# Membrane recursion of a spiking delta-rule layer: from one pass behind the front into the delta loop

## The reference, cut to what matters

```python
def step(carry, ins):
    s, mem = carry
    qt, kt, vt, dt, at, bt = ins
    mem = DECAY * mem + dt                      # DECAY 0.9
    sg = jax.nn.sigmoid(SBETA * (mem - THR))
    hard = (mem > THR).astype(mem.dtype)        # THR 0.5
    spike = sg + jax.lax.stop_gradient(hard - sg)
    mem = mem - spike * THR
    alpha = jax.nn.sigmoid(at + asp * spike)
    beta = jax.nn.sigmoid(bt[..., None] + jnp.sum(spike * bsp, -1, keepdims=True))
    active = (jnp.sum(jnp.abs(spike), -1, keepdims=True) > 0).astype(qt.dtype)
    ...
```

## Time and profile before

| | us |
|---|---|
| median of three runs | 3083.59 |
| the profiled run's own time | 3076.32 |
| its span, first to last instruction | 3074.5 |
| PE busy in the span | 2411.1 (78%) |
| DVE busy | 1566.4 (51%) |
| ACT busy | 994.6 (32%) |
| POOL (GpSimd) busy | 675.6 (22%) |

### The profile page before, as it was taken

How to read it: one execution, slowest core, us unless ns; L and a number is a source line. 1 busy time by engine, 2 the same in 40 slices (tenths; PEclk the granted TensorE clock), 3 DMA queues, 4 the chain that set the end, 5 groups by cost and what they waited for, 6 DMA issues and landing times. The chain is left out here.

```text
span 3074.5 us, 73508 instructions
## 1 busy us (share of the span) xinstructions
PE 2411.1 (78%) x31207; PEld 1690.7 (55%) x31207; DVE 1566.4 (51%) x3747; ACT 994.6 (32%) x1934; POOL 675.6 (22%) x816
## 2 busy tenths in 40 slices
PE   7999889997676530888989898988888868856665
PEld 4666666666655210255656565655566747555553
DVE  4555555554622567364555464636363722584333
ACT  3343443433122530324343434343434332301111
POOL 1000101000044400141313140404040300204553
PEclk9898998987599765789999999999999985556555
DMA  3000000000111102000000000000000011000113
GB/s 142 8 8 1 8 8 5 1 1 1 66 34 34 61 21 120 31 3 19 6 19 6 19 6 19 6 19 6 16 6 2 7 41 46 2 28 29 37 36 104
DMA packets 43654, 79.45 MB, mean 26 GB/s; under 512 B 6116, under 2 KB 27372, under 8 KB 40516
## 3 DMA queue, kind: packets, MB, share of 16 engines
q1 hardware_dynamic: 36292, 60.30, 5.6%
q0 software_dynamic: 7040, 14.43, 1.7%
HBM read 48.56 MB, written 26.15 MB: 24 GB/s over the span
## 5 line engine op out<-in xcount | busy, mean ns | idle before, releaser
L2582 POOL TENSOR_TENSOR delta_scaled_beta_k<-delta_scaled_beta_k,delta_decays 128x256 f32<-128x256 f32 x160 | 124.2, 776 | 537.0 <-DVE weights_sb L2683 363.5
L2661 DVE COPY_PREDICATED delta_neg_a_and_p_t<-delta_level_int,bank 128x256 f32<-128x256 uint8 x384 | 179.6, 538 | 88.5 <-PE bank L2204 87.3
L2228 PEld LDWEIGHTS bank<-delta_inverse,delta_neg_a_and_p_t 64*64 64x64 f32 x5120 | 186.7, 152 | 45.7 <-issue 45.2
L2228 PE MATMUL bank<-delta_inverse,delta_neg_a_and_p_t 64*64 64x64 f32 x5120 | 210.0, 240 | 0.0
L2432 ACT ACTIVATE delta_two_less_ax<-bank 128x512 f32<-128x512 f32 x160 | 94.8, 597 | 248.8 <-PE bank L2228 248.7
L303 PE MATMUL bank<-attn_z_self_t,weights_sb 128*128 128x256 f32 x512 | 149.3, 442 | 14.9 <-DVE attn_cross_values L741 11.2
L2204 PE MATMUL bank<-weights_sb,delta_scaled_beta_k 64*64 64x64 f32 x6144 | 127.7, 228 | 40.2 <-DVE delta_neg_a_and_p_t L2661 35.5
L2204 PEld LDWEIGHTS bank<-weights_sb,delta_scaled_beta_k 64*64 64x64 f32 x6144 | 110.4, 140 | 76.5 <-DVE delta_neg_a_and_p_t L2661 52.3
L683 POOL TENSOR_TENSOR attn_probs<-attn_probs,attn_row_sum 128x512 f32<-128x512 f32 x64 | 65.4, 1043 | 390.6 <-DVE attn_row_sum L766 390.6
L312 PE MATMUL bank<-attn_w_value_out,attn_z_self_t 128*64 128x512 f32 x512 | 144.8, 692 | 2.1 <-DVE attn_z_value_out L706 1.4
L2250 PE MATMUL bank<-delta_two_less_ax,delta_inverse_t 64*64 64x64 f32 x4096 | 133.4, 218 | 3.4 <-issue 3.2
(11 more groups left out here) (508 smaller groups left out, 5527.3 us busy)
## 6 DMA issues: line engine op xcount, KB each, us to landing
delta_spikes<-front_drive SPq DMA_DIRECT2D x8, 1024.0 KB, 8.7
weights_sb<-delta_spikes SPq DMA_DIRECT2D x8, 1024.0 KB, 5.0
weights_sb<-in_w_moe_dram SPq DMA_DIRECT2D x1, 4352.0 KB, 15.3
z_rows<-moe_z_all SPq DMA_DIRECT2D x16, 256.0 KB, 2.3
weights_sb<-moe_outs SPq DMA_DIRECT2D x8, 512.0 KB, 7.2
weights_sb<-in_w_delta_dram SPq DMA_DIRECT2D x1, 2816.0 KB, 9.9
weights_sb<-in_ctx_tok_dram SPq DMA_DIRECT2D x8, 264.0 KB, 5.6
attn_x_channels<-in_x_dram SPq DMA_DIRECT2D x8, 256.0 KB, 3.0
```

The lines of the kernel that those rows point to most:

```text
L2228: last = pe.matmul(out_[rows(sg), u], AP[rows(sg), hp, eo, b4, 0, :], X[rows(sg), hp, u], start=False, stop=True, skip_group_check=True)
L2582: pool.tensor_tensor(r_[:, :, 0, :], r_[:, :, 0, :], a_[:, :, 1, 0:1].to_broadcast([128, T // (2 * c), c]), ALU.mult)
L2661: last = dve.copy_predicated(second(AP[:, hp, eo, :, :, :].rearrange("p b i n -> p (b i) n"), c), m_, PAIR[hp % 2][eo][:, :].rearrange("p ...
```

## The change

The recursion of groups 0 and 1 stays in the front, cut into pieces of 13 time steps that DVE runs behind the convolutions of groups 3 to 7, on 128 x 64 elements. The spikes of group 0 stay in SBUF, those of group 1 go to DRAM. Of the other six groups the front writes the drive itself to DRAM, while it runs. The delta stage loads it two iterations ahead, and in iteration `it` DVE steps the membrane of group `it + 2`, on 128 x 32 elements, in five pieces: 26, 14, 10, 7 and 7 time steps. GpSimd turns the result to spikes behind its last scale. There are two tiles for spikes in place of one, and `kr` has one buffer in place of two.

```diff
-                mem = sb("membrane", [128, NG * HDP * GB], ctx=ctx)
+                mem = sb("membrane", [128, 2 * HDP * GB], ctx=ctx)
...
+                        if g >= 3:
+                            sp.wait_ge(s["drive"], HDP * g)
+                            sp.dma_start(drive_rows[g - 1, :, :, :], drive_of(g - 1)).then_inc(drive_out[(g - 1) % 2], 16)
+                    sp.wait_ge(s["drive"], HDP * NG)
+                    sp.dma_start(drive_rows[NG - 1, :, :, :], drive_of(NG - 1)).then_inc(drive_out[(NG - 1) % 2], 16)
+                    sp.wait_ge(s["spikes"], 2)
+                    sp.dma_start(drive_rows[1, :, :, :], drive_of(1)).then_inc(s["spikes_out"], 16)
...
                             act.wait_ge(s["drive_ps"], HDP * g + j + 1)
-                            act.activation(drive[:, g, j, :], bank[6 + j % 2][:, :], ACT.Copy, scale=2.0).then_inc(s["drive"], 1)
+                            if g >= 4:
+                                act.wait_ge(drive_out[g % 2], 16 * (g // 2 - 1))
+                            act.activation(drive_of(g)[:, j, :], bank[6 + j % 2][:, :], ACT.Copy, scale=2.0).then_inc(s["drive"], 1)
...
-                    dve.wait_ge(s["drive"], NG * HDP)
-                    dr = drive[:, :, :, :].rearrange("p g j (b t) -> p (g j b) t", t=S)
-                    for t in range(S):
-                        m_ = dr[:, :, t]
-                        if t >= 1:
-                            link(dve.scalar_tensor_tensor(m_, mem[:, :], -0.9, m_, ALU.mult, ALU.add))
-                        if t < S - 1:
-                            link(dve.scalar_tensor_tensor(mem[:, :], m_, 1.0, m_, ALU.is_gt, ALU.subtract))
-                    for g in range(NG):
-                        dve.tensor_scalar(drive[:, g, :, :], drive[:, g, :, :], 1.0, None, ALU.is_gt).then_inc(s["spikes"], 1)
+                        if g >= 3:
+                            dve.wait_ge(s["drive"], 2 * HDP)
+                            for t in range(13 * (g - 3), min(13 * (g - 2), S)):
+                                membrane(t)
+                    dve.tensor_scalar(spk0, drive_of(0), 1.0, None, ALU.is_gt).then_inc(s["spikes"], 1)
+                    dve.tensor_scalar(drive_of(1), drive_of(1), 1.0, None, ALU.is_gt).then_inc(s["spikes"], 1)
...
+                    def load_drive(g):
+                        if g >= 2:
+                            sp.wait_ge(s["bt_ps"], nth_of("bt", g - 2, 3))
+                            sp.wait_ge(s["al_rd"], nth_of("al", g - 2, 3))
+                        sp.dma_start(SPK[g % 2][:, :, :], drive_rows[g, :, :, :]).then_inc(s[f"drive_in{g % 2}"], 16)
...
                         out_ = fill("ct", g, j)
-                        pe.wait_ge(s["spikes_in"], 16 * (g + 1))
-                        pe.matmul(out_[:, :], BLOCKSUM, spk[:, j, :], start=True, stop=True).then_inc(s["ct_ps"], 1)
+                        if g == 1:
+                            pe.wait_ge(s["drive_in1"], 16)
+                        elif g >= 2:
+                            pe.wait_ge(s["spikes"], g - 1)
+                        pe.matmul(out_[:, :], BLOCKSUM, SPK[g % 2][:, j, :], start=True, stop=True).then_inc(s["ct_ps"], 1)
...
+                    def spikes(g):
+                        pool.wait_ge(s["potential"], g - 1)
+                        pool.tensor_scalar(SPK[g % 2][:, :, :], SPK[g % 2][:, :, :], 1.0, None, ALU.is_gt).then_inc(s["spikes"], 1)
...
                             scale(it, 4)
+                            if it + 2 < NG:
+                                spikes(it + 2)
...
+                    def membrane(g, t0, t1):
+                        dve.wait_ge(s[f"drive_in{g % 2}"], 16 * (g // 2 + g % 2))
+                        rows_ = SPK[g % 2].rearrange("p h (b t) -> p (h b) t", t=S)
+                        for t in range(t0, t1):
+                            m_ = rows_[:, :, t]
+                            if t == S - 1:
+                                dve.scalar_tensor_tensor(m_, mem[:, :], -0.9, m_, ALU.mult, ALU.add).then_inc(s["potential"], 1)
+                            elif t >= 1:
+                                link(dve.scalar_tensor_tensor(m_, mem[:, :], -0.9, m_, ALU.mult, ALU.add))
+                            if t < S - 1:
+                                link(dve.scalar_tensor_tensor(mem[:, :], m_, 1.0, m_, ALU.is_gt, ALU.subtract))
...
+                        drive = core and it + 2 < NG
+                        if drive:
+                            membrane(it + 2, 0, 26)
                         if tail:
                             t_hidden(it - 1, 0)
...
                         if front:
                             f_bc("bk", it + 1)
+                        if drive:
+                            membrane(it + 2, 26, 40)
                         if tail:
                             t_hidden(it - 1, 2)
...
                         if front:
                             f_bc("bq", it + 1)
+                        if drive:
+                            membrane(it + 2, 40, 50)
+                        if front:
                             f_ct(it + 1, 0)
+                        if drive:
+                            membrane(it + 2, 50, 57)
                         if tail:
                             t_out(it - 1)
+                        if drive:
+                            membrane(it + 2, 57, S)
```

More of the change, by code:

```diff
@@ L1940, in z_rms, with membrane @@
                         last.then_inc(s["z_rms"], 1)
+                    two = drive[:, 0:2, :, :].rearrange("p g j (b t) -> p (g j b) t", t=S)
+                    def membrane(t):
+                        m_ = two[:, :, t]
+                        if t >= 1:
+                            link(dve.scalar_tensor_tensor(m_, mem[:, :], -0.9, m_, ALU.mult, ALU.add))
+                        if t < S - 1:
+                            link(dve.scalar_tensor_tensor(mem[:, :], m_, 1.0, m_, ALU.is_gt, ALU.subtract))
                     z_rms(0)
@@ L1956, in _ @@
                         last.then_inc(s["conv"], 1)
-                    dve.wait_ge(s["drive"], NG * HDP)
-                    dr = drive[:, :, :, :].rearrange("p g j (b t) -> p (g j b) t", t=S)
-                    for t in range(S):
-                        m_ = dr[:, :, t]
-                        if t >= 1:
-                            link(dve.scalar_tensor_tensor(m_, mem[:, :], -0.9, m_, ALU.mult, ALU.add))
-                        if t < S - 1:
-                            link(dve.scalar_tensor_tensor(mem[:, :], m_, 1.0, m_, ALU.is_gt, ALU.subtract))
-                    for g in range(NG):
-                        dve.tensor_scalar(drive[:, g, :, :], drive[:, g, :, :], 1.0, None, ALU.is_gt).then_inc(s["spikes"], 1)
+                        if g >= 3:
[4 more added lines that the diff above has]
+                    dve.tensor_scalar(drive_of(1), drive_of(1), 1.0, None, ALU.is_gt).then_inc(s["spikes"], 1)
             run_stage("front", "bias_row pads gate_w var log_var guessed rstd z_rms z z_rms_ps z_ps z_rms_t z_t g1_ps gate_hidden g2_ps gate conv h "
-                               "h_out0 h_out1 gate_out0 gate_out1 drive_ps drive spikes spikes_out dve", body)
+                               "h_out0 h_out1 gate_out0 gate_out1 drive_out0 drive_out1 drive_ps drive spikes spikes_out dve", body)
         def delta():
@@ L2009, in body @@
                 spare = region[0][:, 11 * 512:]
-                spk = spare[:, 0:HDP * T].rearrange("p (h t) -> p h t", h=HDP)
+                spk1 = sb("odd_spikes", [128, HDP, T], ctx=ctx)
+                SPK = (spare[:, 0:HDP * T].rearrange("p (h t) -> p h t", h=HDP), spk1)
+                mem = sb("membrane", [128, HDP * GB], ctx=ctx)
                 zt = spare[:, HDP * T:HDP * T + T].rearrange("p (i d) -> p i d", d=128)
                 y2 = spare[:, HDP * T + T:HDP * T + 2 * T].rearrange("p (i d) -> p i d", d=128)
-                kr = sb("scaled_beta_k", [128, 2, HDP, T], ctx=ctx)
+                kr = sb("scaled_beta_k", [128, HDP, T], ctx=ctx)
                 al = sb("decays", [128, 2, HDP, T], ctx=ctx)
@@ L2083, in _ @@
                             load_h(g + 3)
-                        if g + 2 < NG:
-                            load_spikes(g + 2)
+                        if g + 3 < NG:
+                            load_drive(g + 3)
                         load_gate(g + 1)
@@ L2190, in diag @@
                                 t = slice(b * S, b * S + S)
-                                last = pe.matmul(two[eo][rows(sg), b4 * 64:b4 * 64 + 64], kr[r, g % 2, hp, t], kq[r, g % 2, 1, hp, t],
+                                last = pe.matmul(two[eo][rows(sg), b4 * 64:b4 * 64 + 64], kr[r, hp, t], kq[r, g % 2, 1, hp, t],
                                                  start=b < 2, stop=True, skip_group_check=True)
@@ L2203, in products @@
                                 t = slice(b * S, b * S + S)
-                                last = pe.matmul(two[eo][rows(sg), b4 * 64:b4 * 64 + 64], kr[r, g % 2, hp, t],
```

(3 more changed lines are left out.)

38 lines of the change are left out of this document (21 added, 17 removed).

## The result

The changed kernel takes 2987.51 us in the median of four runs (2981.93 to 2989.48), the kernel before 3078.35 us on the same chip; the ratio is 0.970 (95% interval 0.967 to 0.972). Measured twice more, each time against the kernel before on the same chip, the ratio was 0.968 (0.962 to 0.973) and 0.968 (0.964 to 0.971); the three pairs of medians lie 91, 103 and 99 us apart. The forecast was 2980 us, range 2960 to 3015. The profiled run took 2981.93 us; its forecast was 2979.

The account below looks back on a forecast made before the run. It took the recursion to stand alone on the path and the delta stage to be PE's, with DVE idle in small gaps. 3076.3 - 108 (front) + 11 (delta) = 2979 us, stated as 2980, range 2960 to 3015.

Parts of the forecast that it names:

- What bounds the kernel: Between front and delta stage DVE's recursion runs alone for 94.6 us; a steady delta group is PE's, 141 of 157 us.
- Price of a small step: DVE membrane step: 0.30 us at 64 columns in the front, 0.23 at 32 in delta; paced 0.33 and 0.264.
- The rule of many small instructions: Skill's advice against many small DVE tiles: recursion work rises from 94.6 to 241 us, losing some 147 us if unhidden.
- The front: End of the front: delta stage starts at about 1118 rather than 1226.2, saving 108 us, between 103 and 110.
- nothing on ACT is late: In the front, ACT takes the last convolution at 1100.2, in its own order, so the pieces delay ACT by nothing.
- The loop: Delta stage: the first piece takes 17.5 us beside GpSimd and overruns its gap, costing 11 us; bounds 0 and 40.
- all but 0.6 us of each lateness passes to PE: Delta stage, first gap: 0.58 us of DVE idle absorbs lateness in each of six groups; 14.9 - 6 x 0.6 = 11 us.
- The sum: Whole program, profiled run: 3076.3 - 108 + 11 = 2979 us, stated as 2980.
- Costed at nothing: Delta stage: GpSimd's spike pass (taken as 5 us), single scaled_beta_k, drive tile loads and the prologue's dropped spike load add nothing.
- Rival 1: Delta stage: meeting GpSimd costs nothing, or the prologue gains a few us by PE's clock; 2962 to 2969 us, chance 0.15.
- rival 2: Delta stage: pieces overrun at 0.3 us or more a step, or PE's clock drops; 2995 to 3020 us, chance 0.22.
- rival 3: Delta stage becomes DVE's at 0.48 us a step, so the kernel is slower; 3090 us and up, chance 0.03.

Follow-up runs that it names:

- the kernel of three instructions: Changed kernel with only three of the 126 DVE recursion instructions left in each of the six loop groups, computing another value; 2970.74 us, ratio 0.964.

## Why the prediction was right, point by point

- **What bounds the kernel.** Right: the recursion stood alone on the path, and the loop is PE's with DVE idle in places. The experiment with 20 more instructions shows the second half: 4.5 us of DVE a group cost no more than the scatter in the third gap.
- **Price of a small step.** 0.30 and 0.23 us forecast, 0.30 and 0.28 in the front, 0.229 and 0.216 in the loop measured, paced 0.33 and 0.258. The column price of 2.2 ns from the wide rows carried over.
- **The rule of many small instructions.** DVE's busy time rose from 1566.4 to 1692.0 us, and the program became 3% shorter. The Trainium skill (VectorE: DVE Perf Modes, section on the TRN2 errata) says that many small tiles each pay a latency that a large one pays once; the busy time agrees, but it prices engine time, not the path.
- **The front.** Forecast -108, measured -106.6 us. One wait was left out: DVE's first piece needs all eight drives of groups 0 and 1, and ACT makes the last of them behind the convolution of group 2. DVE stood 5.8 us for it. So the last convolution ended 94.6 us into the front where 88.6 was forecast, and "nothing on ACT is late" did not hold: ACT's last drive ended 102.3 us into it, where 97.9 was forecast. DVE finished at 104.3 rather than 99 to 102. That the stage ended only 1.6 us later than forecast is partly luck: the prediction allowed 6.5 us for the landing of the last tile, and it took 3.9.
- **The loop.** Forecast +11, measured +13.8 in the mean, of which 9 to 12 are the steps. The mechanism, the first piece meeting GpSimd's squares and scale operations, is shown by moving the squares away: the long steps and the cost go. The piece itself was 16.8 us against 17.5 forecast; the twelve steps beside GpSimd took 6.9 us against 7.2, though not at 0.6 each: three lasted 0.96 and the rest alternated. The size of +11 holds two errors that nearly cancel. The lateness was forecast as 14.9 us in sum; it was 6.6 us in groups 1 to 5 (8.0 and 6.9 in the other profiles) and about 2 in group 0. And the step from there to the path, "all but 0.6 us of each lateness passes to PE", was mis-sized: more was lost than DVE was late, in group 0's iteration about 4 us for 2. PE's waits for the masks, 32 against 23, fit a lateness that is met at several pairs of products; this is argued, and why it grows was not tested.
- **The sum.** The profiled run meets its forecast to 3 us partly by chance: the front gave 1.4 us less and delta cost 4.7 us more than forecast in it, and the unchanged stages before the front were 6.0 us shorter.
- **Costed at nothing.** GpSimd's spike pass: 5.37 us, forecast 5, and with all else that stays in the kernel of three instructions it is within 2 us of nothing. The loads, the single `kr`: no new wait on them in the profile.
- **Rival 1** (the meeting does not matter) fell by the squares on ACT, and its gain in the prologue did not come (granted clock 0.77 against 0.76); **rival 2** (overrun by the pace) by the pace; **rival 3** would have needed 0.48 us a step, where the pace was 0.258 and, over the disturbed first piece, 16.8/51 = 0.33. The granted clock of a steady group stayed at 0.92 to 0.95, against 0.93.

## What to carry to other kernels

A serial chain that stands alone between two stages can be cut and hidden in the gaps of an engine that is not the bound, even if its total work more than doubles (94.6 us to some 237 here); what decides is each gap, so compare piece and gap one by one, and leave a microsecond. Look up what the other engines do in the gap, not only that yours is idle: here GpSimd's squares and scale operations made a 13.0 us piece last 16.8. When stages that did not change scatter by 10 us, judge by the length of the stage that did.

## What the runs showed of the hardware

- A DVE instruction on 128x32, 0.216 to 0.23 us alone, lasts 0.96 to 0.97 us while a GpSimd multiplication of 128x512 (1.04 us) runs, once for each of them; with one tensor input in place of two it lasts as long (0.95 to 0.98 us).
- The step that takes the threshold off lasts 0.192 us on contiguous columns rather than 0.23 with inputs whose columns lie 256 bytes apart.
- GpSimd's comparison of 128x2048 floats with a constant takes 5.37 us, VectorE's 1.22 us.
